# A transformer layer on eight cores: the load of one weight moved to another queue, and half of the evictions of one stage moved to ScalarE

## What is computed

```python
xn = layernorm(x)                                   # x: 2 x 4096 x 2048
x  = x + attention(xn) + ffn(xn)
# attention: q = xn @ w_dq.T @ w_uq.T ; c = xn @ w_dkv.T (512 wide) ; k, v = split(c @ w_ukv.T)
#            16 heads of 128, causal softmax, @ w_out.T
# ffn:       bitlinear(silu(bitlinear(xn, w_gate)) * bitlinear(xn, w_up), w_down), 8192 wide
# bitlinear: activations rounded to 8 bits with a scale per row,
#            weights to -1, 0, 1 with the mean of their absolute values as the scale
```

## Time and profile before

| | us |
|---|---|
| median of 3 timed runs | 5266.7 (5253.9 to 5267.9) |
| profiled execution | 5248.5 |
| its span, slowest core (core 3) | 5246.8 |
| spans of the 8 cores | 5195.3 to 5246.8 |

### The profile page before, as it was taken

How to read it: one execution, slowest core, us unless ns; L and a number is a source line. 1 busy time by engine, 2 the same in 40 slices (tenths; PEclk the granted TensorE clock), 3 DMA queues, 4 the chain that set the end, 5 groups by cost and what they waited for, 6 DMA issues and landing times.

```text
span 5246.8 us, 44503 instructions; the slowest of 8 cores (5195.3 to 5246.8 us)
## 1 busy us (share of the span) xinstructions
PE 3403.4 (65%) x13124; PEld 1240.3 (24%) x13124; DVE 2309.1 (44%) x3060; ACT 901.9 (17%) x918; POOL 157.5 (3%) x250
## 2 busy tenths in 40 slices
PE   3434432586665656665666458788988888349995
PEld 1111110232111211111111113333333333124443
DVE  3444444332142524324251513755566553666554
ACT  3333334124202111120202020000000000210001
POOL 0000000100000000000000001000000000000000
PEclk8656655698656766657567679899999999559997
DMA  5232211785030302212120205744444431435555
GB/s 141 97 128 97 99 70 40 210 267 205 2 122 2 121 26 97 68 56 86 37 99 24 99 1 157 245 133 140 161 160 157 135 128 70 168 121 158 144 143 190
DMA packets 342144, 603.77 MB, mean 115 GB/s; under 512 B 10450, under 2 KB 226002, under 8 KB 304850
## 3 DMA queue, kind: packets, MB, share of 16 engines
q1 hardware_dynamic: 298354, 336.16, 20.7%
q0 software_dynamic: 43360, 262.16, 14.8%
HBM read 554.24 MB, written 50.33 MB: 115 GB/s over the span
## 4 chain that ended last, share of the span: by engine, by line
PE 49%; DVE 19%; issue 15%; DMA 8%; ACT 8%; DVEq 1%; PEldq 0%; ACTq 0%; SPq 0%; POOL 0%; POOLq 0%
PE psp L1062 7%; PE psp L630 4%; PE psb L667 4%; PE psb L922 4%; PE psb L938 4%; PE psb L671 4%; PE psp L922 4%; DVE accTw L399 4%; PE psp L938 4%; PE psp L731 4%; ACT xntb L335 2%; DVE hqfm L1008 2%; ACT hg L928 2%; DVE hstg L905 2%; PE psb L439 2%
## 5 line engine op out<-in xcount | busy, mean ns | idle before, releaser
L1062 PE MATMUL psp<-hqfm,tdq 128*128 128x512 bf16 x2048 | 454.9, 380 | 24.7 <-PE psp L1062 18.0
L655 DVE TENSOR_TENSOR ptile<-ptile,masksb 128x512 bf16<-128x512 bf16 x64 | 27.2, 426 | 875.9 <-ACT ptile L637 875.9
L352 PE MATMUL psp<-identb,xntb 128*128 128x128 bf16 x352 | 93.3, 265 | 476.7 <-ACT xntb L335 273.6
L637 ACT ACTIVATE ptile<-psp 128x1024 bf16<-128x1024 f32 x288 | 294.9, 1024 | 623.0 <-PE psp L630 621.7
L630 PE MATMUL psp<-qfm,kg 128*128 128x512 bf16 x576 | 240.0, 509 | 196.8 <-issue 124.3
L922 PE MATMUL psp<-tgq,xqfm 128*128 128x512 bf16 x1024 | 301.1, 404 | 63.8 <-DVE hstg L905 54.2
L922 PE MATMUL psb<-tgq,xqfm 128*128 128x512 bf16 x1024 | 298.8, 407 | 64.9 <-DVE hstg L905 32.1
L731 PE MATMUL psp<-wukv,ckv 128*128 128x256 bf16 x1152 | 270.0, 382 | 98.3 <-PE psp L731 66.8
L714 PE MATMUL psp<-ckv,wukv 128*128 128x512 bf16 x576 | 173.3, 429 | 196.3 <-issue 134.3
L667 PE MATMUL psb<-ptile,onesb 128*64 128x512 bf16 x576 | 230.2, 491 | 102.1 <-PE psp L630 64.7
L938 PE MATMUL psb<-tuq,xqfm 128*128 128x512 bf16 x1024 | 273.9, 380 | 27.4 <-ACT hg L928 14.7
(11 more groups left out here) (158 smaller groups left out, 4021.0 us busy)
## 6 DMA issues: line engine op xcount, KB each, us to landing
xt<-wdT POOLq DMA_DIRECT2D x64, 1024.0 KB, 5.2
gsq<-wgT SPq DMA_DIRECT2D x64, 1024.0 KB, 6.9
usq<-wuT SPq DMA_DIRECT2D x64, 1024.0 KB, 6.0
dslab<-wdT SPq DMA_DIRECT2D x128, 512.0 KB, 4.1
xt<-wuT POOLq DMA_DIRECT2D x40, 1024.0 KB, 6.0
pa<-wgT POOLq DMA_DIRECT2D x36, 1024.0 KB, 4.9
xt<-xk SPq DMA_DIRECT2D x36, 1024.0 KB, 5.8
hs<-hstg POOLq DMA_DIRECT2D x16, 2048.0 KB, 9.4
```

The lines of the kernel that those rows point to most:

```text
L637: a = S.activation(out=ptile[:, pb, :, :].rearrange("p h c -> p (h c)"), in_=bank2(sp), func=AF.Exp, scale=SCALE, bias=EXPB)
L1062: mm = T.matmul(out=bank(bp + nh), lhsT=tdq[:, hcc, :], rhs=hqfm[:, hcc, nh * 512:(nh + 1) * 512], start=(hcc == 0), stop=(hcc == 63))
```

## The change

The load of wdkv no longer is one converting DMA on POOL's queue. It is two DMAs of float32 on SP's queue, behind xt0 and xt1, each of half of the columns, both into wdst; DVE casts each half into wdkv. The second DMA waits for the first cast. TensorE's wait for the old DMA goes. In P2b the banks 5 and 7 are evicted by ACT, with a Copy activation, and the banks 4 and 6 by DVE as before. The line `wt(S, "mV", vm)` stays behind the loop over the banks. TensorE's waits for a free bank follow the engine that evicted it.

```diff
-        wdkv_dd = dinc(G.dma_start(out=wdkv[:],
-                                   in_=wdkv_d.rearrange("(f p) c -> p f c", p=128)), "g2")
+        for h2 in range(2):
+            sem = "w0" if h2 == 0 else "w1"
+            if h2 == 1:
+                wt(SY, "mV", cnt["mV"])
+            dd = dinc(SY.dma_start(
+                out=wdst[:],
+                in_=wdkv_d[:, h2 * 256:(h2 + 1) * 256].rearrange("(f p) c -> p f c", p=128)), sem)
+            wt(V, sem, dd)
+            inc(V.tensor_copy(out=wdkv[:, :, h2 * 256:(h2 + 1) * 256], in_=wdst[:]), V)
...
-                if gi == 0:
-                    wt(T, "g2", wdkv_dd)
...
-        for b_ in (4, 5, 6, 7):
-            tb_ev[b_] = cnt["mV"]
+        p2b_ev = {b_: ("mV", cnt["mV"]) for b_ in (4, 5, 6, 7)}
...
-                    wt(T, "mV", tb_ev[b])
+                    wt(T, p2b_ev[b][0], p2b_ev[b][1])
...
-                    wt(V, "mT", tm)
-                    ev = V.tensor_copy(
-                        out=hqfm[:, qt * FD + i4 * 4:qt * FD + i4 * 4 + 4, tb * 128:(tb + 1) * 128],
-                        in_=bank(b)[:].rearrange("p (f c) -> p f c", c=128))
-                    tb_ev[b] = inc(ev, V)
+                    dst = hqfm[:, qt * FD + i4 * 4:qt * FD + i4 * 4 + 4, tb * 128:(tb + 1) * 128]
+                    src_b = bank(b)[:].rearrange("p (f c) -> p f c", c=128)
+                    if i4 % 2 == 0:
+                        wt(V, "mT", tm)
+                        p2b_ev[b] = ("mV", inc(V.tensor_copy(out=dst, in_=src_b), V))
+                    else:
+                        wt(S, "mT", tm)
+                        p2b_ev[b] = ("mS", inc(S.activation(out=dst, in_=src_b,
+                                                            func=AF.Copy), S))
                 wt(S, "mV", vm)
```

## The result

The changed kernel is slower: 5392.0 us median against 5281.5 in 37 executions each, taken on several chips. Both medians include executions in which half of the chip's cores ran at a lower clock and took some per cent longer; all ratios and mean spans in this text leave those out. The ratio is then 1.0086 with a 95% interval of 1.0063 to 1.0108, so +45 us (33 to 57) on the 5266.7 of the first table. The profiled execution of the changed kernel took 5310.6 us, 62 more than that of before (5248.5).

The account below looks back on a forecast made before the run. DVE was taken to bound the start (some 4 us to spare) and P2b's 6.43 us step. Load 18.1 plus evictions 42.0 gave 60.1 us: 5308.6 on the profile, 5326.8 on the median, taken as 5321, range 5294 to 5348.

Parts of the forecast that it names:

- part A: Load of wdkv at the start: two plain loads and two DVE casts cost 18.1 us, between 7 and 28.
- part B: Evictions of P2b split between ACT and DVE: a loss of 42.0 us, between 37 and 50.
- The waits of DVE hold all that stands behind them: At the start, DVE's waits for both halves delay tile 0's statistics from 22.96 to 44.6 us.
- The first half: First float32 load of half of wdkv at the start: landed at 30 us, the middle of 24 and 35.
- The term of 18.1 us: Start: the Ln of tile 0 at 45.4 instead of 27.25 us, with nothing earned back.
- ACT's next q2_u behind its evictions: P2b step: q2_u comes only after ACT's evictions, 8.30 us against 6.43, +1.87 in 24 steps, +44.9 us.
- At a new tb: P2b: ACT's q2_u was already on the path, so the split gains 0.87 us, 7 times, -6.1 us.
- The end: End of P2b: dslab loads after ACT's last eviction, first used at +10.3 instead of +7.10: +3.2 us, between 1 and 7.
- The load is free: Rival, start: the load costs nothing as wdkv is first read at 84.5; sum 42 us, chance 0.06.
- much dearer: Rival, start: both halves take 14.8 us each after 35, load over 28 us, sum over 78; chance 0.05.
- Side by side: Rival, P2b: both engines evict in parallel and q2_u stays hidden, 28 us gained, 18 lost, 5257; chance 0.05.
- TensorE's clock: Rival, long stages: a shifted beginning changes the clock; faster needs 76 us, +0.027 in mean clock; chance 0.03.

Follow-up runs that it names:

- e1: Only the load of wdkv changed, P2b as in the kernel before, against that kernel: ratio 0.9994, mean span +12.6 us.
- e3: Kernel before with the split load, a buffer per half, DVE's waits and casts behind tiles 1 and 2: ratio 1.0012, mean span +9.5 us.
- e6: Kernel before plus one DVE wait for the converting load before tile 0: first multiply with wdkv 1.7 to 3.6 us late.
- e4: Kernel before with P2b's evictions split, but the next q2_u of the same tb ahead of ACT's evictions: ratio 0.9895, mean span -29.5 us.
- e9: The changed kernel again, unaltered, against the kernel before on one chip: ratio 1.0174, mean span 5294.7 against 5219.1 us.

## Why the prediction was right

It forecast 5321 us on 5266.7, a loss of 54 to 60; the stages lost 59 by the profile, the first comparison gives 45 (33 to 57) and the second 92. Both mechanisms are as it has them. That its sum of 60.1 lies within about 1 us of the stages' 59 is in part luck: part A was 3 us too dear (18.1 against 14.7 on average), part B 2 us too cheap (42.0 against 44.3). Step by step:

- *The waits of DVE hold all that stands behind them.* Right. The first half was forecast to have landed at 30 and had at 26.8 (core 2); the second wait 9.4 us, was 8.3; casts 2.5 each, were 2.29; Ln at 45.4, was 40.7. The term of 18.1 us was mis-sized: 13.4 on that core and 12.3 to 17.3 on the eight at the first multiply. Most of it is the first half, which landed at 26.2 to 28.8 on the eight cores, while 8.3 to 11.0 for the second has the forecast 9.4 in its middle. 321 GB/s flowed from 10 to 20 us (before: 250), nearer to the 350 that the prediction took for plain loads at a full share than to the 200 of the old start.
- The Trainium skill ("DMA: Bandwidth & Descriptors", Anatomy of one DMA) gives 2.0 us plus the bytes over 436 GB/s for a DMA of GpSimd's queue, which for 2.1 MB makes an estimate of 6.8 us. The two halves went over SP's queue, for which that section has no such price; there the second one kept DVE waiting 8.3 to 11.0 us here and up to 11.5 in e1.
- *ACT's next q2_u behind its evictions.* Right: +1.95 a step instead of +1.87. ACT's bfloat16 copy costs 0.60 as its float32 one does; the missing 0.08 is mostly the gap to q2_u, 0.20 where the rows of neighbouring copies had 0.09. At a new tb the gain was 0.90, forecast 0.87, with q2_u 0.86 after hmax as before. In sum 24 x 1.95 - 7 x 0.90 = 40.5, and 41.0 from first to last cast by the trace, forecast 38.8. (From first to last q2_u it is 43.2, because before the last q2_u ran 2.2 us ahead of the place it now has.)
- The Trainium skill ("ScalarE: Activation LUTs", Rules for kernel authors) gives about 0.3 us and 0.83 ns per element for an activation whose bias is a pointer operand, an estimate of 0.72 us for a bank. The copy's row names no operand beside the bank, so this price is not meant for it, and the trace has 0.60. The rows of this case go in steps of 0.09 us: 2048 columns take 1.91 (statda<-xt), 2.00 with one further operand (q_u<-hbuf,auxs) and 2.09 with two (xntb<-xt,lnt,lnt), and 512 columns 0.60 and, with one, 0.69 (hg<-psb,sgs). The 0.09 between the Silu and the Copy is one such step.
- *The end.* dslab's first use forecast at +10.3, was +10.26, released by its DMA.
- *The rivals.* "The load is free" fell with e1, and e3 and e6 show why; "much dearer" fell with the trace. "Side by side" had the right mechanism for another order: e4 does just that and gains 25 us in the stage, where the rival had 28. The Trainium skill ("PSUM — Partial Sum Buffer", Specifications (TRN2)) says that ScalarE and VectorE read PSUM in parallel at full bandwidth when their banks differ. e4's rows agree: ACT's copy of one bank (4521.08 to 4521.68) and DVE's of another (from 4521.40) overlap, and keep their 0.60 and 0.69 us. It was the order of the list and not PSUM that made the loss. TensorE's clock decided nothing in the stages that changed, but it goes with the scatter that makes two comparisons of the same kernels differ by 47 us.

What stays open: whether the later start changes attention's clock at all. The mean spans of load alone, +12.6 and +14.1, agree with the loss at the start, but with standard errors of 6 and 11 us they would not show a return of under some 10. And the 18 executions of the changed kernel that count in the first comparison have a mean span of 5267.0, only 42 to 48 above before's 5219 to 5225 of the experiments, at a mean clock of 0.759 where the two longer stages alone would give some 0.7565. In e9 the clock was lower, 0.753, and the loss larger. Which of the two is the rule, no run here shows.

## What to carry to other kernels

When work is moved to an idle engine, ask for each moved instruction what stands behind it in that engine's list, and whether the bound engine waits for that; put the producer of the next step ahead of the moved consumers (5.58 us a step against 8.38 for the same instructions). A wait at the head of an engine's list costs all that stands behind it even if its data is not needed for 60 us, once the engine's slack is used up (4 us here); give it a place behind the work that is ready (4.6 us left of 15). Busy shares were better balanced in the slower kernel.

## What was not expected of the hardware

- The span of a core follows its mean granted clock with 3.9 to 4.8 us for each 0.001, depending on the kernel (a straight line through the cores of its executions). The 2.8 us that the prediction took from two cores was too small.
- With the converting load the DMA engines were busier and moved less: 200 GB/s at a share of 0.96 in the first 30 us, against 229 GB/s at 0.77 with plain loads (the same window of the changed kernel, core 2), although the plain loads then waited for DVE. That the neighbours gained by it is not shown: the last constant landed at 14.7 us instead of 12.3, xt0 at 16.9 instead of 17.5 (core 2 against core 3 before).
